# Latent attention: where DVE's inversions and splits stand, how many maxima come early, and the order of keys' passes

## What is computed

```python
c_q = h_t @ W_DQ + b_DQ
c_kv = h_t @ W_DKV + b_DKV
q_c = (c_q @ W_UQ + b_UQ).reshape(b, s, N_HEADS, D_K).transpose(0, 2, 1, 3)
k_c = (c_kv @ W_UK + b_UK).reshape(b, s, N_HEADS, D_K).transpose(0, 2, 1, 3)
v_c = (c_kv @ W_UV + b_UV).reshape(b, s, N_HEADS, D_K).transpose(0, 2, 1, 3)
q_r = (c_q @ W_QR + b_QR).reshape(b, s, N_HEADS, D_HR).transpose(0, 2, 1, 3)
k_r = (h_t @ W_KR + b_KR)[:, None, :, :]
q = jnp.concatenate([q_c, q_r], axis=-1)
k = jnp.concatenate([k_c, k_r], axis=-1)
scores = jnp.einsum('bhsd,bhtd->bhst', q, k) * scale
attn = jax.nn.softmax(scores, axis=-1)
o = jnp.einsum('bhst,bhtd->bhsd', attn, v_c)
return o @ W_O + b_O
```

## Time and profile before

| what | value |
|---|---|
| runs | 4229.01, 4224.52, 4231.56 us; median 4229.01 |
| the profiled execution's own time | 4229.51 us |
| its span | 4227.7 us |
| busy over the span | PE 83%, DVE 70%, ACT 59%, POOL 28% |
| granted TensorE clock, mean | 0.90 of 2.4 GHz |
| latent head loop | 1097 to 1650 us of the span |
| its heads 0 to 7 begin at | 1168.0, 1236.8, 1298.2, 1359.6, 1421.0, 1482.4, 1543.8, 1599.2 us |

### The profile page before, as it was taken

The page is one execution under the profiler, slowest core; times in us unless marked ns, Lnnn a source line. Parts: engine busy times, 40 slices in busy tenths (PEclk is TensorE's granted clock), DMA queues, the critical chain, the costliest instruction groups (busy, mean ns, idle before and its releaser), DMA issues. The chain is left out here.

```text
span 4227.7 us, 85161 instructions
## 1 busy us (share of the span) xinstructions
PE 3529.3 (83%) x32553; PEld 1598.3 (38%) x32557; DVE 2959.5 (70%) x4343; ACT 2514.4 (59%) x4845; POOL 1171.5 (28%) x1183
## 2 busy tenths in 40 slices
PE   5769999672799998879999998589976689999957
PEld 4623333551322223322222224355646322222237
DVE  6467775548676775578999973448975599999833
ACT  3426667355445555338888884344534368888844
POOL 2610000343378882000000000147964300000016
PEclk7869999786899998879999998799997789999979
DMA  3221110210101010010000000320002210000012
GB/s 124 75 74 43 37 42 25 70 52 0 47 19 34 20 30 19 1 66 29 23 32 27 27 14 1 87 75 1 1 1 83 89 36 32 27 27 32 13 58 74
DMA packets 84247, 165.08 MB, mean 39 GB/s; under 512 B 21428, under 2 KB 47684, under 8 KB 82180
## 3 DMA queue, kind: packets, MB, share of 16 engines
q1 hardware_dynamic: 58224, 117.74, 8.9%
q0 software_dynamic: 12704, 22.97, 1.9%
q10 hardware_dynamic: 12916, 18.93, 1.4%
HBM read 112.41 MB, written 35.13 MB: 35 GB/s over the span
## 5 line engine op out<-in xcount | busy, mean ns | idle before, releaser
L1516 DVE TENSOR_REDUCE 32_heads_mx<-32_heads_mps 128x1 f32<-128x1024 f32 x512 | 602.3, 1219 | 48.0 <-PE 32_heads_mps L1366 45.5
L1516 DVE TENSOR_REDUCE 55_heads_mx<-55_heads_mps 128x1 f32<-128x1024 f32 x512 | 602.3, 1219 | 47.2 <-PE 55_heads_mps L1366 44.6
L1486 ACT ACTIVATE 55_heads_p<-55_heads_sps 128x512 f32<-128x512 f32 x1024 | 553.7, 596 | 86.5 <-PE 55_heads_sps L1392 83.2
L1486 ACT ACTIVATE 32_heads_p<-32_heads_sps 128x512 f32<-128x512 f32 x1024 | 553.8, 596 | 86.2 <-PE 32_heads_sps L1392 83.0
L1516 DVE TENSOR_REDUCE 7_heads_mx<-7_heads_mps 128x1 f32<-128x1024 f32 (+7 forms) x384 | 333.5, 908 | 150.8 <-PE 7_heads_mps L1374 103.9
L1486 ACT ACTIVATE 7_heads_p<-7_heads_sps 128x512 f32<-128x512 f32 (+3 forms) x640 | 308.1, 533 | 159.1 <-PE 7_heads_sps L1395 119.1
L2726 DVE TENSOR_REDUCE 21_latent_heads_mx<-21_latent_heads_ring 128x1 f32<-128x1024 f32 x256 | 308.4, 1219 | 133.7 <-PE 21_latent_heads_ring L2530 132.5
L2696 ACT ACTIVATE 21_latent_heads_p<-21_latent_heads_ring,1_latent_heads_tilt_bias 128x1024 f32<-128x1024 f32 x256 | 271.4, 1111 | 198.9 <-PE 21_latent_heads_ring L2556 198.7
L2447 POOL TENSOR_TENSOR 21_latent_heads_psum<-21_latent_heads_psum,21_latent_heads_p 128x1024 f32<-128x1024 f32 x140 | 324.4, 2369 | 0.4
L1392 PE MATMUL 55_heads_sps<-51_head_rows_qs,51_head_rows_ks 123*32 123x512 bf16 x4096 | 314.2, 383 | 9.1 <-ACT 55_heads_p L1486 5.0
L1392 PE MATMUL 32_heads_sps<-30_head_rows_qs,30_head_rows_ks 123*32 123x512 bf16 x4096 | 314.4, 383 | 8.3 <-ACT 32_heads_p L1486 5.0
(11 more groups left out here) (1220 smaller groups left out, 6719.1 us busy)
## 6 DMA issues: line engine op xcount, KB each, us to landing
18_mla_loop_mem_kh<-scratch_latent_keys SPq DMA_DIRECT2D x24, 256.0 KB
3_routed_experts<-in_L0f_experts SPq DMA_DIRECT2D x8, 514.0 KB
9_routed_experts<-in_L0f_experts SPq DMA_DIRECT2D x8, 514.0 KB, 6.5
50_routed_experts<-in_L3f_experts SPq DMA_DIRECT2D x8, 514.0 KB
57_routed_experts<-in_L3f_experts SPq DMA_DIRECT2D x8, 514.0 KB
38_hale_masks_qs<-scratch_q_parts SPq DMA_DIRECT2D x11, 288.0 KB
38_hale_masks_ks<-scratch_k_parts SPq DMA_DIRECT2D x33, 96.0 KB
yT<-scratch_results SPq DMA_DIRECT2D x12, 256.0 KB, 5.8
```

The lines of the kernel that those rows point to most:

```text
L1486: act.activation(pslot[x % PS][:, 0:CW - off], sps[e % SB][:, 0:CW - off], ACT.Exp, scale=SCALE / 2).then_inc(ex_done, 1)
L1516: dve.tensor_reduce(mx[h % 2][:, i, half:half + 1], mps[x % 2][:, 0:w], AX.X, ALU.max).then_inc(mx_taken, 1)
```

## The change

The constants LEAD and FILLED go; SPLIT = 23 comes. (1) `INVERT` becomes steps 11, 13, 15, 17, and with it the division moves from step 16 to 19. (2) `split_max` is cut in two: `join_max` stays behind the last maximum of a head (step 21), the split comes behind the second maximum of the head after (step 23), in head 6 at step 23. (3) Ten maxima of head 1, not four, are made before head 0's scores, and every pair then has two. (4) The keys' pass of a round stands between its two maxima. The banks are dealt anew: the first maximum takes the bank of the previous round's keys, the keys take that of the previous round's first maximum, and the second maximum always the third bank.

```diff
--- before.py
+++ after.py
@@ -2320,11 +2320,10 @@
     AHEAD = 10
     SUMS = 9
     KEPT = 2
-    LEAD = 4
-    FILLED = (AHEAD - LEAD)
     TURNED = 25
+    SPLIT = 23
     LAG = 3
-    INVERT = (11, 12, 13, 14)
+    INVERT = (11, 13, 15, 17)
     DIRECT = 12
     ADDS = DIRECT - 1
     PARTS = 3 * NT
@@ -2384,25 +2383,21 @@
 
         def maxima_at(h, p):
 
-            j = p // 2
-            if h == 0 and j < FILLED:
-                vs = [LEAD + 3 * j] if p % 2 == 0 else [LEAD + 3 * j + 1, LEAD + 3 * j + 2]
-            else:
-                vs = [h * U + p + AHEAD]
-            return [(1 + v // U, v % U) for v in vs if v < U * LASTH]
-
-        STAGE_AT = {4 + 2 * i: i for i in range(STAGED)}
+            v = h * U + p + AHEAD
+            return [(1 + v // U, v % U)] if v < U * LASTH else []
+
+        STAGE_AT = {5 + 2 * i: i for i in range(STAGED)}
         passes = [("keys", 0, 0), ("keys", 0, 1)] + [("max", 0, u) for u in range(2)] + [("keys", 1, 0), ("keys", 1, 1)] + [("max", 0, u) for u in (2, 3)]
         home = [n % RING for n in range(len(passes))]
-        for u in range(4, U):
-            if u in STAGE_AT:
-                passes.append(("keys", KEPT + STAGE_AT[u] // 2, STAGE_AT[u] % 2))
-                home.append((STAGE_AT[u] + 2) % RING)
-            passes.append(("max", 0, u))
-            home.append((home[-1] + 1) % RING)
-        for u in range(LEAD):
-            passes.append(("max", 1, u))
-            home.append((home[-1] + 1) % RING)
+        taken_by_max, taken_by_keys = 0, 2
+        for u in range(4, 4 + 2 * STAGED, 2):
+            i = STAGE_AT[u + 1]
+            passes += [("max", 0, u), ("keys", KEPT + i // 2, i % 2), ("max", 0, u + 1)]
+            taken_by_max, taken_by_keys = taken_by_keys, taken_by_max
+            home += [taken_by_max, taken_by_keys, 1]
+        passes += [("max", 0, u) for u in range(4 + 2 * STAGED, U)] + [("max", 1, u) for u in range(AHEAD)]
+        for n in range(U - 4 - 2 * STAGED + AHEAD):
+            home.append((taken_by_keys, taken_by_max, 1)[(n + 1) % RING])
         named = {home[-3]: 0, home[-2]: 2, home[-1]: 1}
         home = [named[n] for n in home]
         first = 0
@@ -2411,8 +2406,8 @@
                 units = maxima_at(h, 2 * j) + maxima_at(h, 2 * j + 1)
                 passes += [("score", h, 2 * j), ("score", h, 2 * j + 1)] + [("max", *unit) for unit in units]
                 if units:
-                    home += [first, 2] + [1 - first, first, 1 - first][:len(units)]
-                    first = first if len(units) == 3 else 1 - first
+                    home += [first, 2, 1 - first, first]
+                    first = 1 - first
                 else:
                     home += [(2 * j) % RING, (2 * j + 1) % RING]
         place = {which: n for n, which in enumerate(passes)}
@@ -2606,7 +2601,7 @@
                     max_pair(1, u)
                 pe.wait_ge(tilt_copied, 2)
                 turn_max(0)
-                for u in range(2, LEAD):
+                for u in range(2, AHEAD):
                     max_pair(1, u)
                 pe.wait_ge(tilt_scaled, 1)
                 for h in range(MLA_H):
@@ -2725,10 +2720,13 @@
                     dve.wait_ge(mx_ready, U * h + u + 1)
                     dve.tensor_reduce(mx[:, u % NT, u // NT:u // NT + 1], pair_of(("max", h, u))[:], AX.X, ALU.max).then_inc(mx_taken, 1)
 
+                def join_max(h):
+                    dve.wait_ge(mx_taken, U * (h + 1))
+                    dve.tensor_reduce(m, mx[:], AX.X, ALU.max).then_inc(dve_done, 1)
+                    dve.wait_ge(dve_done, LINKS * h + 1)
+
                 def split_max(h):
-                    dve.wait_ge(mx_taken, U * (h + 1))
-                    ch = Chain(dve, dve_done, base=LINKS * h)
-                    ch.link(dve.tensor_reduce(m, mx[:], AX.X, ALU.max))
+                    ch = Chain(dve, dve_done, base=LINKS * h, at=1)
                     by_chunk = mparts[:, 0:PARTS].rearrange("p (c a t) -> p c a t", c=NC, a=3)
                     whole, rest = (at.rearrange("p (c t) -> p c t", c=NC) for at in (m, mrest))
                     split3(ch, dve, [by_chunk[:, :, a, :] for a in range(3)], whole, rest)
@@ -2756,8 +2754,9 @@
                 for u in range(2, U):
                     maximum(0, u)
                 dve.wait_ge(tilt_copied, 2)
+                join_max(0)
                 split_max(0)
-                for u in range(LEAD):
+                for u in range(AHEAD):
                     maximum(1, u)
                 for h in range(MLA_H):
                     for p in range(S):
@@ -2766,7 +2765,11 @@
                                 for unit in maxima_at(h, q):
                                     maximum(*unit)
                                     if unit[1] == U - 1:
-                                        split_max(unit[0])
+                                        join_max(unit[0])
+                                    if unit[1] == 1 and unit[0] > 1:
+                                        split_max(unit[0] - 1)
+                            if h + 1 == LASTH and p == SPLIT:
+                                split_max(LASTH)
                         if h == LASTH and LAG <= p < 2 * DIRECT + LAG and (p - LAG) // 2:
                             add_pair(dve, h, (p - LAG) // 2, (p - LAG) % 2)
                         if h and p in INVERT:
```

## The result

The changed kernel takes 4235.39 us (median of 20 runs, 4228.26 to 4246.67) against 4229.06 (20 runs, 4224.23 to 4236.17): ratio 1.0015, interval 1.0009 to 1.0021. It is 6.3 us longer where 5.3 less were forecast, and lies 2.4 above the range. That is less than the 0.2% which counts as a difference, but the sign is clear. The runs of the changed kernel also spread more, 18 us against 12, and the spread goes with TensorE's mean granted clock over the execution: the four shortest (4228.26 to 4229.66) show 0.898 to 0.900, the five longest (4244.28 to 4246.67) 0.894 or 0.895.

A forecast was written before the change was run, and what follows sets the result against it. PE, partly waiting for DVE, was taken to bound heads 1 to 6, and DVE the keys' rounds. Terms -5.8 - 2.0 - 3.9 + 6.4 = -5.3 took the profiled 4229.51 to 4224.2, by the median 4223.7; range 4214 to 4233.

The forecast's parts named there:

- Inversions, -5.8: Heads 1 to 6: one RECIPROCAL to a pair causes no delay, -0.95 a head, -5.8 us in all.
- limit of 0.86: Heads 1 to 6: DVE work between two pairs is free up to 0.86 us, late beyond it.
- third rival: Heads: the inversions keep costing, half of the -7.8 stays away, the whole takes 4227.6 us; chance 0.13.
- Split, -2.0: Heads 0 to 5: the split one pair later cuts the delay from 0.54 to 0.20 us, -2.0 in all.
- Ten early maxima, -3.9: Before and in head 0: later scores but six pairs lose a maximum, -3.9 us, bounds -2.2 and -5.5.
- Start (+4.5): Ahead of head 0: ten reductions instead of four delay the first score pass by 4.5 us.
- pairs 2 to 5: Head 0: these pairs fall from 4.76 to 3.47 us each, forecast -5.2 in all.
- term for pairs 0 and 1: Head 0: 12.03 us become 8.8, -3.2, of which 1.7 by full clock coming back within pair 0.
- Keys' pass between two maxima, +6.4: Keys' rounds ahead of head 0: 3.72 us each against 3.06, +6.4 us in all, bounds +5 and +8.
- first rival: Keys' rounds fall to half clock for good, 4.99 us each, +1.27 a round, 4236 if all ten; chance 0.12.
- chance of "slower": Whole kernel above 4237.5 us: chance 0.06, said to come from the upper end of the first rival.
- other two rivals: Keys' rounds at DVE's pace, 2.35 us, whole 4210, chance 0.05; inversions that keep costing, whole 4227.6, chance 0.13.

The follow-up runs named there:

- e7: The kernel before with the inversions alone moved to steps 11, 13, 15 and 17; 4304.34 us, ratio to before 0.9990.
- e5: The changed kernel with three unread matmuls behind the second maxima pass of each of the ten keys' rounds; 4304.59 us, ratio to before 0.9995.
- e1: The kernel before with only the moved inversions and the split one tile later; 4224.85 us, ratio to before 0.9981.
- e3: The kernel before with only the keys' pass at its new place and its banks; 4243.72 us, ratio to before 1.0033.
- e2: The kernel before with the ten early maxima alone; 4227.56 us, ratio to before 0.9992.
- e4: The changed kernel with the keys' pass back ahead of its two maxima, with the old banks; 4220.23 us, ratio to before 0.9974.
- e6: The changed kernel with bank 2 always for the first maxima pass and bank 0 for the keys' pass in ten rounds; 4299.54 us, ratio to before 0.9975.
- e10b: The changed kernel once more, unaltered, in another set; 4322.51 us, ratio to before 1.0015.
- e11b: The same kernel as e4, run again beside e10b; 4303.15 us, ratio to before 0.9974.
- e9: e4 with unread matmuls, one in each keys' round and two behind each maximum that follows; 4294.11 us, ratio to before 0.9970.

## Why the prediction was wrong

By its steps:

- **Inversions, -5.8.** Right: -1.01 in each head (e7), -6.1 in six, forecast -0.95 (six times that is 5.7; the prediction wrote 5.8). A reciprocal alone took 0.89 from start to start (1328.40 to 1329.29), 0.03 over the limit of 0.86, and the pairs still came at 3.46: the limit was a little too tight, and the third rival's price did not come.
- **Split, -2.0.** Right: -0.37 a head against -0.34.
- **Ten early maxima, -3.9.** Start (+4.5) and pairs 2 to 5 (-5.1) as forecast. The term for pairs 0 and 1 was mis-sized: -3.2 by a choice of full clock within pair 0, measured -1.3 in the changed kernel, near the -1.5 that the term has without the 1.7 for the clock. Even that is not cleanly the maxima's: with four early maxima the two pairs took 10.69 (e1), 12.03 (before), 12.04 (e3) and 13.35 (e7), by when the clock came back. In the profiles with ten early maxima and no filler behind the rounds (after, e2, e4, e5, e6, e10b, e11b) the two pairs took 10.70 to 11.88; with full clock held by fillers they took 7.60. PE was fed in the stretch ahead, as I wrote, yet a window with 3.72 busy of 4 us (1180 to 1184) showed 0.50 all the same. This alone would have left the forecast in its own range.
- **Keys' pass between two maxima, +6.4, bounds +5 and +8. This is the step that failed.** Its chain was right to 0.01 us (3.71 to 3.72 measured, ACT named) and its sum too at full clock (+6.7 in e5). What failed is that all rounds were put at full clock: with four distances and the twelfth round at or near half the term is +12.1, with all at half +22.3 (e10b). A bound of +8 has room for one half-clock round (1.27) at most.
- **The first rival** named the mechanism and very nearly its price: 4.99 a round forecast, 5.09 and 5.10 measured, and "from the fourth or fifth such round on" the sum changes sign. Its chance of 0.12 was what was wrong. I set against it that the old rounds kept 1.00 with waits of 0.7 us; but waits of 1.5 us were the new thing, and I had no row of full clock kept through such rounds. The new rounds (PE at work for 60% of 3.72 us, by my own figure) lay between a fall behind 1.80 of 4 us and the old rounds with some 2.8 of 4 (windows of before above), so the rows left the question open: an even chance for "some rounds at half" was their reading, and the range should have taken in its 4236 for all ten (4240 with the +22.3 measured). Its "once lost it doesn't come back by such work" was wrong too: within and behind the rounds of the changed kernel the clock came back twice (windows from 1144 and 1192). And the chance of "slower" was said to come from its upper end, but 4236 does not reach the 4237.5 that it needs.
- The other two rivals are out: no round took 2.35, and the inversions cost nothing more. ACT never waited for POOL in head 0.

The Trainium skill (TensorE: Matmul & The Clock Gate, "A second HAM failure mode: psum-queue depth-cycling") spoke of this: gaps between bank groups let the clock swing. The trace now agrees: the clock went from 1.00 to 0.50, back to 1.00 and to 0.50 again within the rounds of the changed kernel (windows from 1132 to 1164), and in e5, with the gaps filled, it stayed at 1.00. The price that the first rival put beside it (+19) lies between the first profile (+12.1) and the second (+22.3).

## What to carry to other kernels

When a step is put where PE must wait longer in each round, cost the round twice, at full and at half clock, and look for a row that keeps full clock with as little work per round; without one, half clock is a likely case and not a rival at 0.12. If two passes of a loop can be given banks so that the slower engine's release is not ahead of both (e6: 3.18 instead of 3.72 from other bank numbers), that can be worth more than the order of the passes (3.18 in the new order, 3.06 in the old). Matmuls whose result nobody reads, put in PE's waits, are a direct test of whether the clock is the cause: e5 got faster by more work, and ACT and DVE had the same to do.

## What was unexpected of the hardware

- The changed kernel, same code and same data, spent four of ten like rounds at or near half clock in one profile (72.39 us for the stretch) and all ten in another (e10b, 82.51); e3, with the same rounds, spent three; with fillers none (66.97). The spread of whole runs is in part this: 18 and 23 us in the two sets of the changed kernel (20 and 12 runs), with mean clocks from 0.885 to 0.900, where the kernel before spread 12 and 18 (20 and 28 runs).
- The way back differs too. At half clock, rounds of the old order came back to 1.00 after one to three of them (e9, e7; e1, e4); those of the new order after two in the first profile and after none in e10b, with PE busy 2.92 to 3.61 of 4 us in the windows shown.
- The chips of the three sets differ by 2% in the kernel before (4231.99 to 4314.96). In the profiles of the first set the first keys' pass comes at 1094 to 1098 us, in the others at 1135 to 1144, at nearly the same mean clock. Some 40 us of it lie in two earlier stages with the same code, the routed ones: from the first instruction on tiles of stage 3 to the first of stage 5 it is 128.8 us in the profile of the kernel before and 149.2 in e11b, from stage 9 to stage 12 it is 132.4 and 152.0. What is slower there was not looked into.
